# The first chunk's rows of a normalised feed-forward kernel, turned by a product instead of a transpose

## What is computed

```python
xn = (x - mean(x)) / sqrt(var(x) + 1e-5)
D = fractal_dimension(xn)                  # one number, from the first 1024 values of xn
x1 = ifft(fft(xn) * filter(D)).real        # a 256x256 circulant product
bits = sigmoid(x1 @ W_el + b_el) > 0.5     # 24 bits a token
attn = x1 + golay_correct(bits) @ W_le + b_le
ffn = gelu(xn @ w1 + b1) @ w2 + b2         # 256 -> 1024 -> 256
out = x + attn + ffn
```

## Time and profile before

| | |
|---|---|
| time, three runs | 407.10, 407.12, 407.69 us; median 407.12 us |
| the profiled execution | 407.3 us, of which 405.5 us are the span of its trace |
| TensorE busy | 400.7 us, 99% of the span |
| VectorE, ScalarE, GpSimd busy | 298.7, 223.3 and 87.2 us |
| granted TensorE clock | 1.00 over the whole span |

### The profile page before, as it was taken

The page is one execution under the profiler, slowest core; times in us unless marked ns, Lnnn a source line. Parts: engine busy times, 40 slices in busy tenths (PEclk is TensorE's granted clock), DMA queues, the critical chain, the costliest instruction groups (busy, mean ns, idle before and its releaser), DMA issues.

```text
span 405.5 us, 5548 instructions
## 1 busy us (share of the span) xinstructions
PE 400.7 (99%) x1774; PEld 329.1 (81%) x1774; DVE 298.7 (74%) x512; ACT 223.3 (55%) x333; POOL 87.2 (21%) x102
## 2 busy tenths in 40 slices
PE   8999999999999999999999999999999999999997
PEld 3888888888888888888888888888888888888886
DVE  5879985878658795677957788476974868757656
ACT  3967556557354664537545474554736556365561
POOL 3142421313003131121313013131121312113000
PEclk9999999999999999999999999999999999999999
DMA  6554333213333213333123332023333031111011
GB/s 187 218 158 156 104 103 106 63 42 104 103 104 98 44 65 103 104 103 97 46 64 104 103 104 90 26 91 103 104 103 78 40 89 53 54 52 52 2 52 52
DMA packets 15307, 35.75 MB, mean 88 GB/s; under 512 B 5440, under 2 KB 6592, under 8 KB 15296
## 3 DMA queue, kind: packets, MB, share of 16 engines
q1 hardware_dynamic: 15152, 35.49, 27.4%
q10 hardware_dynamic: 144, 0.13, 0.1%
HBM read 27.17 MB, written 8.45 MB: 88 GB/s over the span
## 4 chain that ended last, share of the span: by engine, by line
PE 97%; DMA 1%; DVE 1%; POOL 0%; SPq 0%; issue 0%
PE p_h L964 43%; PE p_f L982 28%; PE p_f L987 14%; PE p_s L1030 5%; PE p_l L1017 4%; PE p_s L1038 2%; DMA x_sb<-x 1%; PE p_f L997 0%; SPq L248 0%; DVE stats L830 0%; POOL row_nums L361 0%; DVE rows_sb L817 0%; PE p_g L1006 0%; PE p_l L1006 0%; PE p_s L1139 0%
## 5 line engine op out<-in xcount | busy, mean ns | idle before, releaser
L446 ACT ACTIVATE h<-p_h,small_sb 128x512 f32<-128x512 f32 x128 | 88.2, 689 | 139.4 <-PE p_h L964 138.9
L633 DVE TENSOR_TENSOR h_lo<-h,h_hi 128x512 fp32r<-128x512 f32 x128 | 102.9, 804 | 69.2 <-ACT h_hi L454 69.2
L982 PE MATMUL p_f<-h_hi,w_hi 128*128 128x512 f32 x252 | 98.3, 390 | 0.0
L982 PE MATMUL p_f<-h_hi,w_lo 128*128 128x512 f32 x252 | 98.1, 389 | 0.0
L369 POOL TENSOR_TENSOR uv<-xn 128x512 f32<-128x512 f32 x30 | 59.3, 1996 | 126.0 <-DVE xn L618 126.0
L454 ACT CAST h_hi<-h 128x512 fp32r<-128x512 f32 x128 | 79.5, 621 | 5.8
L964 PE MATMUL p_h<-xT_hi,w_hi 128*128 128x512 f32 (+1 forms) x258 | 79.4, 389 | 0.0
L964 PE MATMUL p_h<-xT_lo,w_hi 128*128 128x512 f32 (+1 forms) x258 | 79.2, 388 | 0.0
L964 PE MATMUL p_h<-xT_hi,w_lo 128*128 128x512 f32 (+1 forms) x258 | 79.0, 387 | 0.0
L987 PE MATMUL p_f<-h_lo,w_hi 128*128 128x512 f32 x252 | 77.6, 389 | 0.0
L964 PEld LDWEIGHTS p_h<-xT_lo,w_hi 128*128 128x128 f32 x258 | 48.3, 188 | 10.3 <-DVE xT_lo L839 0.2
(11 more groups left out here) (127 smaller groups left out, 325.2 us busy)
## 6 DMA issues: line engine op xcount, KB each, us to landing
xt_sb<-xt SPq DMA_DIRECT2D x16, 512.0 KB, 5.3
x_sb<-x SPq DMA_DIRECT2D x15, 512.0 KB, 4.6
rows_sb<-rows_dram SPq DMA_DIRECT2D x15, 512.0 KB, 4.4
out<-xt_sb SPq DMA_DIRECT2D x15, 512.0 KB, 2.8
xt_sb<-w SPq DMA_DIRECT2D x3, 512.0 KB, 7.5
xt_sb<-w SPq DMA_DIRECT2D x2, 256.0 KB, 4.5
x_sb<-x SPq DMA_DIRECT2D x2, 128.0 KB, 2.1
x_sb<-x SPq DMA_DIRECT2D x1, 256.0 KB, 3.2
```

The source lines that it names most:

```text
L446: nc.scalar.activation(h[m % 2][:], p_h[:, m % 2, :], ACT.Gelu, bias=small_sb[:, S_B1 + m:S_B1 + m + 1]).then_inc(gelu_done, 1)
L633: nc.vector.tensor_tensor(h_lo[m % HR][:], h[m % 2][:], h_hi[m % HR][:].bitcast(F32), ALU.subtract).then_inc(h_lo_done, 1)
L982: mm(p_f[:, a, :], w[:, m, a * HF:(a + 1) * HF], h_hi[r][:], start=(m == 0 and w is w2_hi), stop=False, skip_group_check=True)
```

## The change

- `normalise` is split. `centre_rows(g)` on VectorE only subtracts the mean and waits for the statistics alone; the inverse deviation goes into a diagonal matrix a tile, the identity times `row_nums`, made by two ScalarE instructions a group (`deviations(g)`, into `by_dev`, a view of `uv`).
- `turn_rows(g)` replaces the transposes: four float32 matrix products of a centred tile (stationary) with its diagonal (moving).
- The identity is made on GpSimd (`affine_select` on `ones`) and no longer loaded.
- The first quarter of w1 is loaded and split as two single blocks; each engine's list of steps changes accordingly. On ScalarE `gelu(0, 1)` also moves ahead of `w2_part_hi(0)`.
- `first_ups()` replaces `up(0, 0, 0)` and `up(0, 0, 1)`: both are made by halves of 256 tokens, with the second group's `turn_rows(1)` between the first group's high products and the rest, and both hidden blocks end with the second group's low products.
- Chunk 1's rows are loaded ahead of the first load of w2, and its statistics stand ahead of `hidden_lo(0, 0)` on VectorE instead of behind `hidden_lo(0, 1)`. The third small sum moves from behind `down(0, 1)` to behind `down(0, 2)`. `IDLE` goes from 12 to 10.

```diff
-W1_PARTS = ((0, 2), (2, 4), (4, 6), (6, MB))
-W1_LOADS = ((0, 2), (2, 4), (4, MB))
+W1_PARTS = ((0, 1), (1, 2), (2, 4), (4, 6), (6, MB))
+W1_LOADS = ((0, 1), (1, 2), (2, 4), (4, MB))
...
-IDLE = 12
+IDLE = 10
...
+        by_dev = uv[:, :, :].rearrange("p a (j t) -> p (a j) t", t=P)[:, 0:CT, :]
...
-            sp.dma_start(id_sb[:], ident).then_inc(id_in, 16)
             load_w1(0)
+            load_w1(1)
             sp.dma_start(small_sb[:], small).then_inc(small_in, 16)
-            load_w1(1)
+            load_w1(2)
             sp.dma_start(con[:], consts).then_inc(con_in, 16)
+            load_x(1)
             load_w2(0)
-            load_x(1)
-            load_w1(2)
+            load_w1(3)
             load_w2(1)
             sp.dma_start(basis_sb[:, :, :], basis.rearrange("(k p) e -> p k e", p=P)).then_inc(basis_in, 16)
...
+            pool.wait_ge(pool_set, 3)
+
+            nc.gpsimd.affine_select(out=id_sb[:], in_=ones[:], pattern=[[1, P]], base=0, channel_multiplier=-1,
+                                    compare_op=ALU.is_equal, fill=0.0).then_inc(id_made, 1)
...
-            w1_part_hi(0)
-            for g in range(2):
+            def deviations(g):
+
+                act.wait_ge(rstd_done, g + 1)
+                for j in range(g * HALF, (g + 1) * HALF):
+                    last = nc.scalar.mul(by_dev[:, j, :], id_sb[:], row_nums[0][:, 1, j:j + 1])
+                last.then_inc(dev_made, 1)
+
+            def turned_rows_hi(g):
                 act.wait_ge(t0_done, g + 1)
                 nc.scalar.copy(half_tokens(xT_hi[0], g), half_bank(g)).then_inc(t0_hi, 1)
+
+            act.wait_ge(id_made, 1)
+            deviations(0)
+            w1_part_hi(0)
+            turned_rows_hi(0)
             w1_part_hi(1)
+            deviations(1)
+            turned_rows_hi(1)
+            w1_part_hi(2)
             act.wait_ge(small_in, 16)
             gelu(0, 0, first=True)
             hidden_hi(0, 0, first=True)
+            gelu(0, 1, first=True)
             w2_part_hi(0)
-            gelu(0, 1, first=True)
             hidden_hi(0, 1, first=True)
-            w1_part_hi(2)
+            w1_part_hi(3)
             gelu(0, 2, first=True)
             hidden_hi(0, 2, first=True)
             w2_part_hi(1)
-            w1_part_hi(3)
+            w1_part_hi(4)
             gelu(0, 3, first=True)
             hidden_hi(0, 3, first=True)
             w2_part_hi(2)
...
-            def normalise(g):
-
-                dve.wait_ge(rstd_done, g + 1)
+            def centre_rows(g):
+
+                dve.wait_ge(stat_done, g + 1)
                 for j in range(g * HALF, (g + 1) * HALF):
-                    last = nc.vector.tensor_scalar(xn0[:, j, :], x_sb[0][:, j, :], mv[0][:, j, 0:1],
-                                                   row_nums[0][:, 1, j:j + 1], ALU.subtract, ALU.mult)
+                    last = nc.vector.tensor_scalar(xn0[:, j, :], x_sb[0][:, j, :], mv[0][:, j, 0:1], None, ALU.subtract)
                 last.then_inc(xn0_done, 1)
-
 
             for j in range(HALF):
                 dve.wait_ge(x_first[j], 16)
...
             last.then_inc(stats_made, 1)
             dve.wait_ge(stats_made, 1)
             aggregate(0, range(HALF))
+            centre_rows(0)
             dve.wait_ge(x_in[0], 16)
             for j in range(HALF, CT):
                 last = nc.vector.bn_stats(stats[:, j, :], x_sb[0][:, j, :])
             last.then_inc(stats_made, 1)
             dve.wait_ge(stats_made, 2)
             aggregate(0, range(HALF, CT))
+            centre_rows(1)
             for g in range(2):
-                normalise(g)
-            w1_part_lo(0)
-            for g in range(2):
+                w1_part_lo(g)
...
             nc.vector.tensor_reduce(fr_s[:, 0, :], fr_a[:], AX.X, ALU.add).then_inc(part_sums, 1)
+            statistics(1, 1)
+            dve.wait_ge(stats_made, 3)
+            aggregate(1)
             hidden_lo(0, 0)
...
             hidden_lo(0, 1)
-            statistics(1, 1)
-            dve.wait_ge(stats_made, 3)
-            aggregate(1)
             hidden_lo(0, 2)
...
-                        pe.wait_ge(*((w1_hi_ready, 1) if n == 0 else (w1_ready, n + 1)))
-                if not (first and m < 2):
-
-                    pe.wait_ge(gelu_done, MB * c + m - 1)
-
-                groups = 2 if first and m == 0 else 1
-                for g in range(groups):
-                    tok = slice(g * CTOK // groups, (g + 1) * CTOK // groups)
-                    n = 0
-                    for w, xp in ((w1_hi, xT_hi), (w1_lo, xT_hi), (w1_hi, xT_lo)):
-                        if groups == 2:
-
-                            if w is w1_lo and g == 0:
-                                pe.wait_ge(w1_ready, 1)
-                            elif w is w1_hi:
-                                pe.wait_ge(t0_hi if xp is xT_hi else t0_lo, g + 1)
-                        for k in range(KB):
-                            last = mm(p_h[:, m % 2, tok], w[:, k, m * P:(m + 1) * P], xp[par][:, k, tok],
-                                      start=(n == 0), stop=(n == 3 * KB - 1))
-                            n += 1
+                        pe.wait_ge(w1_ready, n + 1)
+
+                pe.wait_ge(gelu_done, MB * c + m - 1)
+
+                n = 0
+                for w, xp in ((w1_hi, xT_hi), (w1_lo, xT_hi), (w1_hi, xT_lo)):
+                    for k in range(KB):
+                        last = mm(p_h[:, m % 2, :], w[:, k, m * P:(m + 1) * P], xp[par][:, k, :],
+                                  start=(n == 0), stop=(n == 3 * KB - 1))
+                        n += 1
                 last.then_inc(up_done, 1)
+
+            def turn_rows(g):
+
+                pe.wait_ge(xn0_done, g + 1)
+                pe.wait_ge(dev_made, g + 1)
+                for k in range(KB):
+                    for j in range(HALF):
+                        last = mm(half_bank(g)[:, k, j * P:(j + 1) * P], xn0[:, g * HALF + j, k * P:(k + 1) * P],
+                                  by_dev[:, g * HALF + j, :], start=True, stop=True, skip_group_check=True)
+                last.then_inc(t0_done, 1)
+
+            def half_up(m, g, terms, last_term=2):
+
+                tok = slice(g * GTOK, (g + 1) * GTOK)
+                for n in terms:
+                    w, xp = ((w1_hi, xT_hi), (w1_lo, xT_hi), (w1_hi, xT_lo))[n]
+                    for k in range(KB):
+                        last = mm(p_h[:, m, tok], w[:, k, m * P:(m + 1) * P], xp[0][:, k, tok],
+                                  start=(n == 0 and k == 0), stop=(n == last_term and k == KB - 1), skip_group_check=True)
+                return last
+
+            def first_ups():
+
+                turn_rows(0)
+                pe.wait_ge(t0_hi, 1)
+                for m in range(2):
+                    pe.wait_ge(w1_hi_ready, m + 1)
+                    half_up(m, 0, (0,))
+                turn_rows(1)
+                pe.wait_ge(w1_ready, 1)
+                half_up(0, 0, (1,))
+                pe.wait_ge(t0_lo, 1)
+                half_up(0, 0, (2,))
+                half_up(1, 0, (2,), last_term=1)
+                pe.wait_ge(w1_ready, 2)
+                half_up(1, 0, (1,), last_term=1)
+                pe.wait_ge(t0_hi, 2)
+                half_up(0, 1, (0, 1))
+                half_up(1, 1, (0, 1))
+                pe.wait_ge(t0_lo, 2)
+                half_up(0, 1, (2,)).then_inc(up_done, 1)
+                half_up(1, 1, (2,)).then_inc(up_done, 1)
...
-            pe.wait_ge(id_in, 16)
-            for g in range(2):
-
-                pe.wait_ge(xn0_done, g + 1)
-                for k in range(KB):
-                    for j in range(HALF):
-                        last = nc.tensor.transpose(half_bank(g)[:, k, j * P:(j + 1) * P],
-                                                   xn0[:, g * HALF + j, k * P:(k + 1) * P], id_sb[:])
-                last.then_inc(t0_done, 1)
-
             pe.wait_ge(pool_set, 3)
-            for m in range(LOOK):
+            first_ups()
+            for m in range(2, LOOK):
                 up(0, 0, m, first=True)
                 if m == 2:
                     summed_over(0, NS, fr_s[:, 0, :], part_sums, fr_summed)
...
                 down(0, m, first=True)
                 if m == 0:
                     summed_over(8, NS, fr_s[:, 2, :], part_counts, fr_counted)
-                if m == 1:
+                if m == 2:
                     summed_over(16, 1, fr_d[:, 0:1], logged, dim_made)
...
```

## The result

The changed kernel takes 412.71 us (median of 6 runs, 410.91 to 413.66) against 407.23 us (6 runs, 407.10 to 407.69): ratio 1.0127, 95% interval 1.0101 to 1.0153. That is 5.5 us slower, where +1.2 was forecast, and outside the range. The execution that was profiled took 413.63 us.

A forecast was written before the change was run, and what follows sets the result against it. The prediction took TensorE to bound the kernel: a start plus a stream of products without a hole. Mark +1.07 and VectorE/w1 +0.1 give +1.17 us on 407.12, so 408.3 us; range 407.4 to 409.8.

The forecast's parts named there:

- the start: TensorE up to the third hidden block: later second turn and uncovered first gelu delay `up(0, 0, 2)` by +1.07 us.
- The dimension chain: Third small sum through GpSimd's polynomial and ScalarE's basis to the circulant: cost 0, up to +0.3 us if a step slips.
- The delay of the angle: VectorE's answer to the third small sum, moved behind `down(0, 2)`: 22.2 us instead of 20.31, 1.9 later.
- the slack: Between GpSimd and ScalarE: `filt_w` was ready at 26.20 us and ScalarE took it only at 27.50.
- The clock: Rival 2, chance 0.10: TensorE's clock rises late; 0.9 us more if only the first turn is slow, about 2.7 at most.
- the mark: Start of `up(0, 0, 2)`, the third hidden block, on TensorE: 11.68 us before, forecast about 12.75, +1.07 us.
- the gelu's wait: TensorE ahead of `up(0, 0, 2)`: both blocks end together, so it waits 0.6 to 0.8 us for gelu 0.
- the identity: Made on GpSimd at the start, 0.15 to 1.7 us inside about 2.1 us of room: costs nothing.
- the early chunk 1: Chunk 1's rows loaded ahead of w2's first half, which lands later but in time; chunk 1 gains time nobody waits for.
- the +0.1 that was forecast on VectorE: Chunk 1's statistics ahead of `hidden_lo(0, 0)`, room 0.2 us before `down(0, 0)`; with w1's fourth part, +0.1 us for the two.
- The price of a float32 product by the circulant's row: Each turn on TensorE: two products of 128 columns are four instructions, 0.45 us; four take 0.9, about 1.07 with latency.
- The factor of four: Rival 3, chance 0.05: a float32 turn product costs four transposes, 0.9 us more in each turn, +1.8 us.

The follow-up runs named there:

- the last version above: Changed kernel with transposes of normalised rows, twelve zeros, third sum in its old place, first hidden block finished before the second's low products: 407.72 us, ratio 1.0012 against kernel before.

## Why the prediction was wrong

It had the direction, and the mechanism of the start, but +1.17 us of 5.5. With the third sum in its old place and twelve zeros the changed kernel takes 408.85 us, inside the range; two other losses took it out.

- **The dimension chain, "Cost 0, up to +0.3 if a step slips", is the step that failed.** The delay of the angle was right (1.9 us; 1.6 measured), and so was the slack: with the polynomial at 5.05 us and the sum late the circulant did not wait. But the polynomial's 5.2 us was taken as fixed. By the count above it held 2.3 us of waiting for VectorE's instructions already; moved 1.6 us later it met the centring and the scaling of chunk 1 too, lost 4.3 us, and its end moved by 3.6. Measured: +1.8 us alone in the kernel before, 2.1 in the changed one. This is enough by itself: the two runs of the changed kernel that the clock spared, 410.91 and 411.40 us, are outside the range.
- **The clock was a rival with a chance of 0.10, and it came.** Dropping two zeros was costed at nothing, as the way to free TensorE in time. Four of six runs of the changed kernel (412.67 to 413.66) paid for it, two (410.91, 411.40) did not, and 1.7 us of the median is its share. Its price at the far end was given as 2.7 us; the runs of the kernel with the sum back show 2.65. What was wrong is how often, and the place of the risk: filling the later holes changed nothing, two more zeros did. The rows also bounded the rise more closely than "between 6 and 8.3 us": the four transposes at 6.66 us took 0.63 us, like the later ones' 0.66, where four that began at the lower rate took 0.87 (at 6.38 us, in the kernel with transposes back). Why one execution has the early clock and the next has not stays open.
- **The start**: +1.07 at the mark was forecast, +1.57 measured once both other losses are repaired (13.25 against 11.68). The order of events was right in each point: first turn at 6.24 (5.95 forecast), second at 9.03 (8.7) with the diagonals as its releaser, the gelu's wait 0.69 us, the mark 13.25 (12.75). The terms were 0.3 us too small for the first turn, which began when its last diagonal was there, 6.09 us, and about 0.2 for the rest. In the time it is 408.85 against 407.16, +1.7 where 1.17 was forecast. Of this the product with its diagonals is 0.8 us, the order that leaves the gelu uncovered 0.3, and 0.5 to 0.6 stay with the halves and whatever else the last version above shares with the changed kernel; this last part was not taken apart further.
- **Right at about nothing**: the identity (407.26 us) and the early chunk 1 (407.31), both against 407.17 and not told apart from it by their intervals, which leave room for the +0.1 that was forecast on VectorE. The loads of w1 by single blocks were not run alone. The price of a float32 product by the circulant's row held: 1.13 us for eight instructions, 1.07 forecast. The factor of four that the Trainium skill names ("TensorE: Matmul & The Clock Gate", Terms) did not show: a turn is eight instructions in 1.13 us against four in 0.63 for the transposes, a factor of two in instructions at the same step.
- The parts are 1.7 (start) + 2.1 (sum) + 1.7 (clock, at the median) = 5.5. They are steps from one kernel to the next, so that they add up to the measured 5.5 proves nothing; that the sum costs 1.8 to 2.1 us in three separate pairs of kernels does.

## What to carry to other kernels

A slack read from one trace holds only with the same neighbours: before a chain on GpSimd is moved, look at what VectorE will be doing beside its new place, and price its steps with the rows that already overlap such instructions; here the trace of the kernel before had five of them. Products on zeros ahead of the first real work are not filler to be trimmed to the microsecond; let them run to the first real product, which made the late clock rarer here but did not end it, and judge them by the spread of many executions, since one profile can show either case. Splitting work so that two results finish together can uncover what had run between them, here a gelu of 0.69 us.

## What had not been expected of the hardware

The granted clock of the profile did not show the first low stretch: in the changed kernel it reads 1.00 everywhere while a step of 128 columns in float32 takes twice its later time. It shows a fall after a first rise (0.50 from 8 to about 11.4 us in the kernel with eight zeros). The steps between the starts of products are the safer sign.
